# A kernel's beginning: prologue blocks folded into the first sublayer, transfers issued from two queues, and the opening's matmuls reordered

## The chip, the cores and the metric

The kernel runs on one core of a Trainium2 chip. The metric is the device time of one execution in microseconds (us); smaller is better. TensorE (PE) multiplies matrices and transposes by multiplying with an identity, VectorE (DVE), ScalarE (ACT) and GpSimd (POOL) work on elements, and SyncE (SP) issues transfers (DMA). Each engine runs its own instruction stream and waits for others on semaphores. The traces show TensorE's clock at two levels, 1.2 and 2.4 GHz; the granted clock of a stretch is given as a share of the higher one.

## What is computed

Input is `x`, 8 batches of 256 tokens with 256 features, in float32. A chain of residual sublayers is applied:

1. latent attention (16 heads): layer norm, projection to latents of 192 (query) and 64 (key and value) columns and 64 rotary columns, RMS norm of the latents, attention with a causal mask, output projection;
2. a linear layer whose weight is made ternary: `scale = mean(|W|)`, then every weight is rounded to one of -scale, 0, +scale;
3. a gated delta rule sublayer with short convolutions;
4. the ternary linear layer again;
5. latent attention again with other weights (in the code: call 1), and after it two smaller attention and feed-forward sublayers.

The kernel absorbs weights: the query weight and the key weight of a head are multiplied once into `wq0`, `wq1` (64 latent columns), and the value and output weights once into `w_out`, so that the attention works on latents. `layout` on the host only rearranges the inputs; it computes no product of them.

## The kernel before, in words

`build` makes its blocks one after the other. A `Block` gives each engine its stream; at its end all engines meet in a barrier, and the next block starts after it.

- `load_inputs` (line 134) is the first block: SP issues three transfers, the first batch `x[:, 0]`, the identity `ident` and the causal `mask`, all counted on one semaphore. DVE waits for all three and casts the identity to bfloat16 (line 150); the cast is used by the delta rule sublayer alone. POOL sets the constants `minus_half` and `ones_row`. The engines also prime the signals (each `Signal` is a semaphore with a counter that starts ahead, so that "the buffer of two iterations ago is free" holds at the beginning).
- `prime_signals` (line 279) is the second block: POOL alone primes the 13 preparation signals and 15 loop signals of the attention, 28 semaphore increments. Nothing else happens in it.
- `mla_sublayer` (line 332) with `call` = 0 is the third block: attention 0 with the ternary layer between its batches and the opening of the delta rule near its end. With `call` = 1 it is run again after the delta rule (there `after_attention` is false: each batch first goes through the ternary layer, then through attention 1).

Only the start of `mla_sublayer` matters here. SP issues its transfers in this order: `w_lat`, `norm_w` (the semaphore `small_in`), six tables (`small_in`), the ternary bias, the ternary weight (the float weight `w` in call 0, the finished weight `w_ste` from a DRAM buffer in call 1), the four query weights `q_nope`, `k_nope`, `q_pe0`, `q_pe1` (`queries_in`), `w_v`, `w_o` (`outputs_in`), then in call 0 the other seven batches and the weights of the next sublayer.

The dependent chain of call 0 for batch 0 is: layer norm (DVE L173 to L179, POOL power L197, DVE L189), transposes on PE (L213), copy on ACT (L664), latent projections (PE L656, ACT L673), squares (ACT L676, L678), root mean square (DVE L600 to L603, POOL L634 and L638), normalisation (DVE L612, L615) and the copy of the values (DVE L709). PE then transposes the normalised latents (`prep_late_pe`, L688 to L693). Beside this runs the preparation of weights:

- `query_weights_pe` (L544): 32 matmuls with 64 columns each, in two halves, into banks 1 to 4. A float32 matmul counts as two instructions in the profile. `query_weights_dve` (L554) copies the four banks to `wq0`, `wq1`. `query_weights_pool` (L561, L563) copies the rotary parts into them; it waits for `queries_in`.
- the ternary weight in call 0: row sum (DVE L512), total over partitions by one matmul with ones (PE L507) into bank 0, then eight DVE steps (L519 to L536). They use `w_out` as scratch (`z`, `up`, `down`, `wt`), so `output_weights_act` waits for the last step.
- `output_weights_pe` (L576) multiplies `w_v` and `w_o` of 16 heads into four banks (5, 6, 7, 1), and ACT copies them to `w_out` (L586).

PE's order in call 0 is: transposes and latents of batch 0, first half of the query weights, transposes of the latents, second half, total of the ternary weight, output weights, `weights_ready_pe` (a wait for all prepared weights), `project_pe` for head pairs 0 and 1 (L723, L724), then the loop over 64 head pairs: `scores_pe` (L762, L764), `project_pe` two pairs ahead, values times probabilities, output projection, transposes of the probabilities (L795). DVE turns each projection with the rotary tables (`rope_dve`, L730 and L736), POOL adds (L746), and ACT copies the other half (`abs_act`, L752). DVE takes masked maxima of the scores (L203) and ACT the exponentials (L783). In call 1 PE begins with the ternary layer of batch 0 (transposes, `ternary_y_pe` L491), and the ternary layer of batch 1 stands between the second half of the query weights and the output weights.

DVE's order in call 0 is: layer norm of batch 0, row sum, RMS norm, values, the eight steps, the four copies of the query weights, `rope_dve` 0 and 1, the loop. POOL's order is: two memsets (L1092, L1093), ones, power of the layer norm (L197), rotary part of the keys and the powers of the RMS norm, the copies L561 and L563, the rotary additions.

## Time and profile before

| what | us |
|---|---|
| median of 3 runs (3353.66 to 3354.33) | 3354.06 |
| the profiled execution, its own time | 3349.63 |
| span of that execution in the trace | 3347.8 |
| PE busy in the span | 3202.3 (96%) |
| DVE busy | 2408.9 (72%) |
| ACT busy | 1946.7 (58%) |
| POOL busy | 820.8 (25%) |

The mean granted clock of the profiled execution is 0.99. A line of the trace's timeline gives the start and the duration in us, engine, line of the kernel, operation, output and inputs, and in brackets how long the engine had been idle and what ended that. PE is the matmul, PEld its weight load, SPq the issue of a transfer on SP. Where equal operations follow each other, they are merged, and the duration is that of the whole group. A line of transfers gives the size and the median time from issue to landing.

### The profile page before, as it was taken

To read this page: it belongs to the slowest core of one execution; us is meant where nothing else is said; L and a number is where in the kernel's file an instruction comes from. 1 tells how busy PE (TensorE), PEld (TensorE's weight loads), DVE (VectorE), ACT (ScalarE), POOL (GpSimd) and SP (SyncE) were. 2 spreads that over 40 slices of the span, in tenths; PEclk is the share of its full clock that TensorE was granted. 3 is DMA by queue.
4 is the path that set the end of the run, shared out by engine and by line. 5 is a ranking of instruction groups with operands and counts; after the bars stand their busy time and mean duration, and the time that the engine had idled before them with its cause. 6 is when DMAs were issued, how large, how long until landed. Compare 5 with 4: busy or idle time off the path is not lost. (4 is left out here: it accounts for less than half of the span.)

```text
span 3347.8 us, 89254 instructions
## 1 busy us (share of the span) xinstructions
PE 3202.3 (96%) x34218; PEld 2635.2 (79%) x34218; DVE 2408.9 (72%) x7923; ACT 1946.7 (58%) x4769; POOL 820.8 (25%) x828
## 2 busy tenths in 40 slices
PE   6999989999999999999999969999889999999999
PEld 5888878888888888888888848888667777777787
DVE  4777778777788777788777637777666777777764
ACT  3555556666666666666666626565455555555553
POOL 2333322222222222222222323333210111111100
PEclk9999999999999999999999989999999999999999
DMA  6000000000000000000000040000000000000000
GB/s 241 1 1 1 1 8 27 21 21 17 17 18 25 18 25 18 15 21 21 21 22 18 12 162 1 1 1 1 1 1 1 2 1 1 1 5 5 5 8 10
DMA packets 51338, 66.84 MB, mean 20 GB/s; under 512 B 4962, under 2 KB 40291, under 8 KB 49379
## 3 DMA queue, kind: packets, MB, share of 16 engines
q1 hardware_dynamic: 50914, 61.13, 5.7%
q8 instruction: 274, 4.49, 0.5%
q14 instruction: 150, 1.22, 0.1%
HBM read 58.56 MB, written 2.56 MB: 18 GB/s over the span
## 5 line engine op out<-in xcount | busy, mean ns | idle before, releaser
L1404 DVE SCALAR_TENSOR_TENSOR d_acc<-d_raw,d_taps,d_acc 128x255 f32<-128x255 f32 x1116 | 627.4, 603 | 127.7 <-ACT d_raw L1392 114.5
L2482 ACT ACTIVATE s_probs<-s_probs,s_nmax 128x128 f32<-128x128 f32 (+1 forms) x768 | 287.0, 446 | 176.9 <-DVE s_nmax L203 176.2
L1659 ACT COPY d_power<-bank 128x768 f32<-128x768 f32 x320 | 259.0, 810 | 216.3 <-PE bank L1652 216.3
L203 DVE CUSTOM_DVE_ANT_0 s_probs<-bank,mask 128x128 f32<-128x128 f32 (+1 forms) x768 | 225.5, 349 | 108.0 <-PE bank L2463 107.9
L746 POOL TENSOR_TENSOR a_q<-a_rope 64x512 f32<-64x512 f32 x128 | 164.8, 1288 | 533.7 <-DVE a_recip L814 314.0
L1390 ACT ACTIVATE d_acc<-bank,d_tap_bias,d_taps 128x256 f32<-128x256 f32 x372 | 189.9, 561 | 162.9 <-PE bank L1368 156.4
L783 ACT ACTIVATE a_area<-a_area,a_nmax 128x128 f32<-128x128 f32 (+1 forms) x512 | 226.4, 443 | 85.7 <-DVE a_nmax L203 84.9
L203 DVE CUSTOM_DVE_ANT_0 a_area<-bank,mask 128x128 f32<-128x128 f32 (+1 forms) x512 | 159.0, 355 | 133.3 <-PE bank L764 130.8
L809 ACT COPY a_area<-bank 128x512 f32<-128x512 f32 (+1 forms) x260 | 137.2, 580 | 117.4 <-PE bank L800 117.4
L736 DVE TENSOR_TENSOR a_rope<-bank,a_sinT 32x512 f32<-32x512 f32 x256 | 177.4, 693 | 5.6
L1804 POOL TENSOR_TENSOR d_o_rs<-d_o_var,minus_half 128x4 f32<-128x4 f32 x64 | 69.6, 1087 | 402.3 <-DVE d_o_var L1798 402.3
L1432 POOL TENSOR_TENSOR d_qT<-d_acc,d_sigm 128x512 f32<-128x512 f32 x62 | 82.3, 1327 | 328.0 <-ACT d_sigm L1414 328.0
L723 PE MATMUL bank<-a_latT,a_wq 128*128 128x256 f32 x512 | 153.9, 382 | 6.9 <-DVE a_rope L736 4.5
L2490 PE MATMUL bank<-ident,s_probs 128*128 128x128 f32 x1152 | 147.6, 274 | 7.4 <-ACT s_probs L2482 4.7
L724 PE MATMUL bank<-a_qT,a_wq 128*128 128x256 f32 x512 | 153.7, 382 | 0.0
L764 PE MATMUL bank<-a_latT,a_q 128*128 128x256 f32 x512 | 153.6, 382 | 0.0
L2490 PEld LDWEIGHTS bank<-ident,s_probs 128*128 128x128 f32 x1152 | 130.3, 141 | 22.5 <-ACT s_probs L2482 15.2
L855 PE MATMUL bank<-a_w_out,a_area 128*128 128x256 f32 x512 | 145.6, 407 | 1.7 <-DVE a_area L844 1.7
L197 POOL TENSOR_TENSOR rstd<-var_eps,minus_half 128x2 f32<-128x2 f32 x64 | 46.1, 720 | 397.9 <-DVE var_eps L179 393.2
L1652 PE MATMUL bank<-d_power 64*64 64x64 f32 x4096 | 142.3, 217 | 0.0
L730 DVE TENSOR_TENSOR a_rope<-bank,a_cosT 64x512 f32<-64x512 f32 x128 | 88.9, 694 | 73.1 <-PE bank L724 71.2
L2590 PE MATMUL bank<-s_xT,m_w_up 128*128 128x256 f32 x512 | 140.3, 396 | 0.0
(287 smaller groups left out, 8621.7 us busy)
## 6 DMA issues: line engine op xcount, KB each, us to landing
d_alpha<-d_alpha_rows SPq DMA_DIRECT2D x64, 256.0 KB, 3.6
d_g_decay<-d_running_rows SPq DMA_DIRECT2D x32, 258.0 KB, 3.5
a_w_o<-in_a_w_o SPq DMA_DIRECT2D x2, 2048.0 KB, 16.8
a_area<-in_a_q_nope SPq DMA_DIRECT2D x2, 1536.0 KB, 8.2
x<-in_x SPq DMA_DIRECT2D x8, 256.0 KB, 16.8
d_wk<-in_d_wk SPq DMA_DIRECT2D x1, 2048.0 KB
d_wq<-in_d_wq SPq DMA_DIRECT2D x1, 2048.0 KB
d_wv<-in_d_wv SPq DMA_DIRECT2D x1, 2048.0 KB
```

The source lines that it names most:

```text
L203: return core.nc.vector.tensor_tensor_reduce(out=out, in0=scores, in1=core.mask[:, blocks], scale=-1.0, scalar=HIGHEST, op0=ALU.add, op1=A ...
L723: nc.tensor.matmul(out, wq0[:, h], latT[:, it % 2, 0], start=True, stop=False)
L724: last = nc.tensor.matmul(out, wq1[:, h], qT1[:, it % 2], start=False, stop=True)
L736: last = nc.vector.tensor_tensor(rope2[other], b_q[rows, :].rearrange("p (j t) -> p j t", j=2), sinT[rows].rearrange("p (j t) -> p j t", j ...
L746: nc.gpsimd.tensor_tensor(q[CL:P, n % 2], rope1[CL:P], rope2[CL:P], ALU.add)\
L764: nc.tensor.matmul(out[:, P:3 * P], q[:, n % 2, j, P:T], keys, start=False, stop=True, skip_group_check=True).then_inc(g.scores_in_psum.se ...
L783: last = nc.scalar.activation(own, own, ACT.Exp, scale=-1.0, bias=nmax[:, h % AHEAD, t:t + 1], accum_out=sums[:, n % 2, j, t:t + 1])
L1390: nc.scalar.activation(convolved(G, r)[:, j], b_proj[:, j * T:(j + 1) * T], ACT.Identity, scale=taps[:, r // 2, h, 3:4], bias=tap_bias[:, ...
L1404: last = nc.vector.scalar_tensor_tensor(out=convolved(G, r)[:, j, d:T], in0=raw[:, r % 2, j, 0:T - d], scalar=taps[:, r // 2, h, 3 - d:4 - ...
L1659: nc.scalar.copy(power[:], b_step[:, :, 0:3 * P]).then_inc(g.step_out, 1)
L2482: last = nc.scalar.activation(own, own, ACT.Exp, scale=-1.0, bias=nmax[:, s % 2, t, i:i + 1])
L2490: last = nc.tensor.transpose(heads[:, i, n * P:(n + 1) * P], probs[:, s % 2, i, n * P:(n + 1) * P], core.ident[:])
```

## The change

The two prologue blocks go. What they did moves into the first block of `mla_sublayer` (call 0): SP issues the first batch and the identity ahead of everything; the mask comes after the query weights; each input has a semaphore of its own, so DVE waits for the first batch alone before the layer norm, PE for the identity before the transposes, and DVE for the mask before the loop. PE primes the 28 signals. POOL sets its constants in the same stream. The cast of the identity moves to `set_up_dve`, near the end of attention 0.

Transfers come from two queues, in both calls. SP: `w_lat`, `norm_w`, query weights, now with the tables `cosT` and `sinT` among them, in call 0 the mask and the ternary bias, then the output weights. ACT: the four small tables and, in call 0, the ternary weight after them; in call 1 the finished ternary weight and the bias ahead of them.

The ternary weight's total is computed in bank 7 (`b_y`) instead of bank 0, right after the latents of batch 0. `output_weights_pe` comes after `project_pe` 0 and 1 and ACT's copies after `abs_act` 0 and 1, with bank 2 in place of bank 1; the wait for `w_out` moves to the first transposes of the loop.

The diff (lines left out are context):

```diff
@@ -66,7 +66,10 @@
         self.bank = [self.banks[:, i] for i in range(8)]
-        self.ready = ctx.enter_context(nc.semaphore("constants_ready"))
+        self.first_tokens_in = ctx.enter_context(nc.semaphore("first_tokens_in"))
+        self.ident_in = ctx.enter_context(nc.semaphore("ident_in"))
+        self.mask_in = ctx.enter_context(nc.semaphore("mask_in"))
+        self.constants_set = ctx.enter_context(nc.semaphore("constants_set"))
@@ -131,39 +134,35 @@
-def load_inputs(core):
-    nc, ins = core.nc, core.ins
-    with nc.Block() as block:
-        @block.sync
-        def _(sp):
-            sp.dma_start(core.x[:, 0], ins["x"][0]).then_inc(core.ready, 16)
-            sp.dma_start(core.ident[:], ins["ident"][:]).then_inc(core.ready, 16)
-            sp.dma_start(core.mask[:], ins["mask"][:]).then_inc(core.ready, 16)
-        @block.vector
-        def _(dve):
-            for s in (core.ln_stats, core.ln_mv, core.ln_var, core.ln_out):
-                s.prime(dve, 1)
-            core.x_updated.prime(dve, 2)
-            dve.wait_ge(core.ready, 16 * 3)
-            nc.vector.tensor_copy(core.ident_bf[:], core.ident[:])
-        @block.gpsimd
-        def _(pool):
-            core.ln_rstd.prime(pool, 1)
-            nc.gpsimd.memset(core.minus_half[:], -0.5)
-            nc.gpsimd.memset(core.ones_row[:], 1.0)
-        @block.scalar
-        def _(act):
-            core.xnT_ready.prime(act, 1)
-        @block.tensor
-        def _(pe):
-            core.xnT_in_psum.prime(pe, 1)
+def load_inputs_sp(core, sp):
+    sp.dma_start(core.x[:, 0], core.ins["x"][0]).then_inc(core.first_tokens_in, 16)
+    sp.dma_start(core.ident[:], core.ins["ident"][:]).then_inc(core.ident_in, 16)
+def prime_dve(core, dve):
+    for s in (core.ln_stats, core.ln_mv, core.ln_var, core.ln_out):
+        s.prime(dve, 1)
+    core.x_updated.prime(dve, 2)
+def prime_pool(core, pool):
+    core.nc.gpsimd.memset(core.minus_half[:], -0.5).then_inc(core.constants_set, 1)
+    pool.wait_ge(core.constants_set, 1)
+    core.nc.gpsimd.memset(core.ones_row[:], 1.0).then_inc(core.constants_set, 1)
+    pool.wait_ge(core.constants_set, 2)
+    core.ln_rstd.prime(pool, 1)
+def prime_pe(core, pe, prepared, looped):
+    core.xnT_in_psum.prime(pe, 1)
+    for s in prepared:
+        s.prime(pe, 1)
+    for s in looped:
+        s.prime(pe, 2)
@@ -277,19 +276,6 @@
-def prime_signals(core, prepared, looped):
-    with core.nc.Block() as block:
-        @block.gpsimd
-        def _(pool):
-            for s in prepared:
-                s.prime(pool, 1)
-            for s in looped:
-                s.prime(pool, 2)
@@ -301,6 +287,7 @@
         self.loaded, self.ones_set = sem("t_loaded"), sem("t_ones_set")
+        self.w_in = sem("t_w_in")
@@ -403,9 +390,9 @@
         tables = [(cos_tok[:], "cos_tok"), (sin_tok[:], "sin_tok"), (ms_scale[:], "ms_scale"),
-                  (q_scale[:], "q_scale"), (cosT[:], "cosT"), (sinT[:], "sinT")]
-        queries = [(q_nope, "q_nope"), (k_nope[:], "k_nope"), (q_pe0, "q_pe0"),
-                   (q_pe1, "q_pe1")]
+                  (q_scale[:], "q_scale")]
+        queries = [(q_nope, f"{tag}q_nope"), (k_nope[:], f"{tag}k_nope"), (q_pe0, f"{tag}q_pe0"),
+                   (q_pe1, f"{tag}q_pe1"), (cosT[:], "cosT"), (sinT[:], "sinT")]
@@ -440,7 +427,7 @@
             pool.wait_ge(*core.ln_out(ternary_at(b), NT))
-            pool.wait_ge(tern.loaded, 32 * (call + 1))
+            pool.wait_ge(tern.loaded, 16 if after_attention else 48)
@@ -485,7 +472,7 @@
             else:
-                pe.wait_ge(tern.loaded, 32 * (call + 1))
+                pe.wait_ge(tern.loaded, 48)
@@ -503,12 +490,11 @@
             pe.wait_ge(tern.row_sum_ready, 1)
-            pe.wait_ge(*g.latT_ready(-1, 2))
-            nc.tensor.matmul(b_prep[:, 0:1], ones[:], row_sum[:], start=True, stop=True)\
+            nc.tensor.matmul(b_y[:, 0:1], ones[:], row_sum[:], start=True, stop=True)\
...
         def ternary_row_sum_dve(dve):
-            dve.wait_ge(tern.loaded, 32)
+            dve.wait_ge(tern.w_in, 16)
@@ -516,7 +502,7 @@
             dve.wait_ge(tern.sum_in_psum, 1)
-            nc.vector.tensor_scalar(scale[:], b_prep[:, 0:1], 1.0 / (D * D), None, ALU.mult)\
+            nc.vector.tensor_scalar(scale[:], b_y[:, 0:1], 1.0 / (D * D), None, ALU.mult)\
@@ -563,13 +549,13 @@
-        OUT_BANKS = (5, 6, 7, 1)
+        OUT_BANKS = (5, 6, 7, 2)
...
             for n, bank in enumerate(OUT_BANKS):
-                if bank == 1:
-                    pe.wait_ge(g.wq_ready, 4 * call + 1)
+                if bank == 7 and after_attention:
+                    pe.wait_ge(tern.weight_step, 1)
@@ -586,9 +572,8 @@
-        def weights_ready_pe(pe):
+        def query_weights_ready_pe(pe):
             pe.wait_ge(g.wq_ready, staged)
-            pe.wait_ge(g.w_out_ready, staged)
@@ -788,6 +773,8 @@
             h = 2 * n + j
+            if h == 0:
+                pe.wait_ge(g.w_out_ready, staged)
@@ -870,18 +857,16 @@
             def _(sp):
+                if after_attention:
+                    load_inputs_sp(core, sp)
...
                     sp.dma_start(dst, ins[f"{tag}{name}"][:]).then_inc(g.small_in, 16)
-                for dst, name in tables:
-                    sp.dma_start(dst, ins[name][:]).then_inc(g.small_in, 16)
-                sp.dma_start(t_bias[:], ins["f0_b"].rearrange("(o n) d -> o n d", o=1)
-                             .broadcast_to([P, 1, D])).then_inc(tern.loaded, 16)
+                for dst, name in queries:
+                    sp.dma_start(dst, ins[name][:]).then_inc(g.queries_in, 16)
                 if after_attention:
-                    sp.dma_start(w[:], ins["f0_w"][:]).then_inc(tern.loaded, 16)
-                else:
-                    sp.dma_start(w_ste[:], tern.w_rows).then_inc(tern.loaded, 16)
-                for dst, name in queries:
-                    sp.dma_start(dst, ins[f"{tag}{name}"][:]).then_inc(g.queries_in, 16)
+                    sp.dma_start(core.mask[:], ins["mask"][:]).then_inc(core.mask_in, 16)
+                    sp.dma_start(t_bias[:], ins["f0_b"].rearrange("(o n) d -> o n d", o=1)
+                                 .broadcast_to([P, 1, D])).then_inc(tern.loaded, 16)
@@ -898,23 +883,26 @@
             def _(pe):
-                if not after_attention:
+                if after_attention:
+                    prime_pe(core, pe, g.prep, g.loop)
+                    pe.wait_ge(core.ident_in, 16)
+                else:
...
                 prep_lat_pe(pe, -1, range(NT))
+                if after_attention:
+                    ternary_sum_pe(pe)
...
                 query_weights_pe(pe, 1)
-                if after_attention:
-                    ternary_sum_pe(pe)
-                else:
+                if not after_attention:
...
                     ternary_y_pe(pe, 1)
-                output_weights_pe(pe)
-                weights_ready_pe(pe)
+                query_weights_ready_pe(pe)
...
                 project_pe(pe, 1)
+                output_weights_pe(pe)
@@ -959,7 +947,10 @@
             def _(dve):
-                if not after_attention:
+                if after_attention:
+                    prime_dve(core, dve)
+                    dve.wait_ge(core.first_tokens_in, 16)
+                else:
@@ -980,6 +971,8 @@
                 rope_dve(dve, 1)
+                if after_attention:
+                    dve.wait_ge(core.mask_in, 16)
@@ -1037,16 +1030,26 @@
             def _(act):
-                if not after_attention:
+                if after_attention:
+                    core.xnT_ready.prime(act, 1)
+                else:
+                    act.dma_start(w_ste[:], tern.w_rows).then_inc(tern.loaded, 16)
+                    act.dma_start(t_bias[:], ins["f0_b"].rearrange("(o n) d -> o n d", o=1)
+                                  .broadcast_to([P, 1, D])).then_inc(tern.loaded, 16)
+                for dst, name in tables:
+                    act.dma_start(dst, ins[name][:]).then_inc(g.small_in, 16)
+                if after_attention:
+                    act.dma_start(w[:], ins["f0_w"][:]).then_inc(tern.w_in, 16)
+                else:
...
                     ternary_copy_act(act, 1)
-                output_weights_act(act)
...
                 abs_act(act, 1)
+                output_weights_act(act)
@@ -1089,6 +1092,8 @@
             def _(pool):
+                if after_attention:
+                    prime_pool(core, pool)
@@ -1259,6 +1264,8 @@
         def set_up_dve(dve):
+            dve.wait_ge(core.ident_in, 16)
+            nc.vector.tensor_copy(core.ident_bf[:], core.ident[:])
@@ -2792,8 +2799,6 @@
         ternary = Ternary(ctx, core)
-        load_inputs(core)
-        prime_signals(core, mla.prep, mla.loop)
```

## Rows read from the trace of the kernel before

**Rows 1.** Busy time by 2 us stretches: columns PE, PEld, DVE, ACT, POOL, granted clock, DMA share, GB/s.
```profile
4.00:6.00 2.00, 0.00 (x0) 0.00 (x0) 0.23 (x1) 0.00 (x0) 0.00 (x0) 1.00 0.03 12
...
50.00:52.00 2.00, 2.00 (x8) 1.64 (x7) 0.00 (x0) 0.00 (x0) 0.79 (x1) 0.62 0.98 418
```

**Rows 2.** Timeline of the opening: start us, duration us, engine and line, idle before.
```profile
0.73 0.39 SPq L140 DMA_DIRECT2D x<-in_x  x1
...
7.61 1.80 POOL L1092 MEMSET a_wq<- 64x2048 f32 x1 [6.45 <-POOLq L282]
...
7.65 0.75 DVE L173 BATCH_NORM_STATS2 stats<-x 128x6 f32<-128x256 f32 x2 [2.74 <-PEq L282]
...
8.72 0.72 DVE L179 TENSOR_SCALAR var_eps<-mean_var 128x2 f32<-128x2 f32 x1
...
10.21 0.71 POOL L197 TENSOR_TENSOR rstd<-var_eps,minus_half 128x2 f32<-128x2 f32 x1
```

**Rows 3.** Transfers of the opening: first tokens' landing, an issue, output weights' landing.
```profile
DMA to landing us min/median/max: 2.6/16.8/17.1
...
12.25 0.43 SPq L884 DMA_DIRECT2D a_area<-in_a_q_nope  x1
...
a_w_o<-in_a_w_o SPq DMA_DIRECT2D x1, 2048.0 KB, 17.7
```

**Rows 4.** Timeline from the latents' norm to the first scores' maxima.
```profile
23.49 0.20 POOL L638 TENSOR_TENSOR a_inv_rms<-a_inv_rms,a_q_scale 128x4 f32<-128x4 f32 x1
...
24.90 0.23 DVE L709 COPY a_values<-a_k_tok 128x128 f32<-128x128 f32 x1
...
26.82 5.57 PE L544 MATMUL bank<-a_k_nope,a_area 128*128 128x64 f32 x32 [6.71 <-DMA a_rope<-in_a_q_pe]
...
26.82 1.04 POOL L561 COPY a_wq<-a_q 128x1024 f32<-128x1024 f32 x1 [3.13 <-DMA a_rope<-in_a_q_pe]
...
36.77 2.81 PE L576 MATMUL bank<-a_w_o,a_w_v 128*64 128x256 f32 x24
...
36.87 0.16 DVE L519 TENSOR_SCALAR a_t_scale<-bank 128x1 f32<-128x1 f32 x1 [11.75 <-PE bank L507]
...
40.95 2.46 DVE L554 COPY a_wq<-bank 128x512 f32<-128x512 f32 x4
...
43.51 1.04 PE L723 MATMUL bank<-a_latT,a_wq 128*128 128x256 f32 x2 [0.73 <-DVE a_wq L554]
...
47.15 0.69 DVE L730 TENSOR_TENSOR a_rope<-bank,a_cosT 64x512 f32<-64x512 f32 x1 [3.73 <-PE bank L724]
...
54.23 0.29 DVE L203 CUSTOM_DVE_ANT_0 a_area<-bank,mask 128x128 f32<-128x128 f32 x1
```

**Rows 5.** Two lines of VectorE over the whole span: duration ns min/median/max.
```profile
L1404 DVE SCALAR_TENSOR_TENSOR d_kT<-d_raw,d_taps,d_kT x12: 453/478/1498, 445.3 to 456.1; 128x255 f32<-128x255 f32 x4, 128x254 f32<-128x254 f32 x4, 128x253 f32<-128x253 f32 x4
...
L179 DVE TENSOR_SCALAR var_eps<-mean_var x64: 168/171/717, 8.7 to 3224.5; 128x2 f32<-128x2 f32 x64
```

**Rows 6.** The second attention call's start: timeline, and landing of the ternary weight.
```profile
1958.28 0.58 ACT L480 COPY xnT<-bank 128x512 f32<-128x512 f32 x1 [10.83 <-PE bank L213]
...
1962.26 3.50 PE L491 MATMUL bank<-a_t_w_ste,xnT 128*128 128x256 f32 x8 [4.02 <-DMA a_t_w_ste<-t_w_ste_rows]
...
a_t_w_ste<-t_w_ste_rows SPq DMA_DIRECT2D x1, 256.0 KB, 4.7
...
1989.41 3.67 PE L576 MATMUL bank<-a_w_o,a_w_v 128*64 128x256 f32 x32
...
1993.82 0.67 PE L723 MATMUL bank<-a_latT,a_wq 128*128 128x256 f32 x2 [0.73 <-issue]
...
2000.07 0.60 PE L764 MATMUL bank<-a_latT,a_q 128*128 128x256 f32 x2
...
2000.65 1.28 ACT L783 ACT_TABLE_LOAD   x1
...
2002.21 0.29 DVE L203 CUSTOM_DVE_ANT_0 a_area<-bank,mask 128x128 f32<-128x128 f32 x1
```

## The prediction

> **What bounds the kernel now.** I read the share of busy time first, then the 2 us stretches and the timeline of the two openings of the attention, then the landings. Over the whole span PE is the busiest engine; but the change touches only the first 60 us and the first 50 us of the second attention call, so the price has to be read there. In these stretches no engine is the bound: a chain of dependent steps is, and once the loop over head pairs runs, all that follows waits for data alone. So an opening that is shorter by some us moves the end by as many. The point that I follow is the start of the first masked maximum of the loop, 54.23 in call 0 [rows 4] and 2002.21 in call 1 [rows 6].
>
> Of call 0 the reader should see four things. The first batch was issued at 0.73 and lands 2.6 later, at 3.33 [rows 2, 3], but DVE reads it at 7.65, released by the priming on POOL and the barrier; in between the DMA engines are 3% busy [rows 1, 2]. PE starts the query weights at 26.82, when the last query transfer lands, though the values were copied at 24.90 [rows 4]. The ternary weight's steps begin at 36.87, 11.75 after DVE ran out of work, because the total stands behind both halves of the query weights on PE; the copies of the query weights (40.95, 2.46 long) queue behind these steps, and the first projection behind the copies, at 43.51 [rows 4]. And that projection takes 3.64 (until 47.15), where the same one in call 1 takes about 2.05: PE had idled, and the granted clock is 0.62 around 51 [rows 1, 4].
>
> **Call 0, part by part.**
>
> *Barriers and priming go.* DVE's layer norm starts at 3.35 instead of 7.65: 4.30 earlier. PE now makes the 28 increments, ACT five issues and a table load; both are waited for only after 6, so they cost nothing as long as they take less than 5 us (an issue takes 0.43 [rows 3]). The constants on POOL and its memsets (1.80 and a short one [rows 2]) start at about 0.8 and end before 4. Before, the last step of the norm's variance took 717 ns beside that memset, against a median of 171 [rows 5], and POOL reached the power only at 10.21. Now the variance starts at 3.35 + 1.07 = 4.42 and takes 0.17, and the power starts at 4.66: 5.55 earlier. From there to the end of the latents' norm nothing changes: POOL's last scale would end at 23.69 - 5.55 = 18.14, and the norm at 24.90 - 5.55 = 19.35. The identity and `w_lat` are issued within the first 2 us; nothing waits for them.
>
> *Queries.* The first query transfer was issued at 12.25 and PE started at 26.82, 14.57 later [rows 3, 4]. It is now fifth on SP, 0.73 + 4 x 0.45 = 2.55. The bias and the ternary weight no longer stand ahead, which helps; the latents' weight is still under way and two tables of 128 KB are added, which hurts. I take the same 14.57 and get 17.1, with 15 and 19 as ends. PE's row from 26.82 to the output weights at 36.77 is 9.95 without a gap, of which 0.3 is the total that has moved ahead; so the query weights end at 17.1 + 9.65 = 26.75. That includes the transposes of the latents, whose inputs are there by then.
>
> *The total moved.* It costs PE 0.3 at about 15, where PE waits for the queries anyway. Bank 7 is free then. DVE no longer idles for it: the ternary steps follow the values' copy. From 36.87 to 40.95 they take 4.08, and the copies 2.46 [rows 4].
>
> *A new collision.* POOL's two copies (1.04 and about the same [rows 4]) ran while DVE idled. Now they start at 18.2 together with DVE's norm, whose operations read two tensors from SBUF. What that costs is seen elsewhere: an operation of this form has a median of 478 ns and a maximum of 1498 [rows 5], so it can wait a whole POOL operation out. The bounds are 0 and 2.07. I take 2.07, since the same scale releases both engines and POOL's copy is one step from starting. The norm then ends at 21.4, the values at 21.65, the ternary steps at 25.75, the copies at 28.2, and the first projection starts at 28.3 instead of 43.51. The last bank of PE's own chain (26.75 + 0.6) is ready just before. The Trainium skill ("SBUF — State Buffer", SBUF: two separate sides) says that whoever starts first holds the shared port for the whole instruction; were DVE first, POOL would wait, the projection would start at 27.4, and the sum would be 0.9 better.
>
> *Output weights moved behind the projections.* From the first projection to the first maximum call 1 needs 2002.21 - 1993.82 = 8.39 [rows 6]: projection, rotary, projection, rotary, at 2.05 and 2.13 each. Now the 32 output matmuls, 3.67 [rows 6], stand on PE between the second projection and the scores, beside the second rotary, and the scores of one head (0.60 and the 128-column pair, 0.8) come after. New chain at the high clock: 2.05 + 2.13 + 2.05 + 3.67 + 0.8 + 0.1 = 10.8. The output weights' inputs took 17.7 from issue; even at that they land well before 36. With the low clock for the first projection alone it is 12.4; with the low clock throughout 3.64 x 2 + 2.13 + 7.34 + 1.6 = 18.35. PE idles 1.5 us before the first projection and had idled before it in the old kernel, so I take 12.4. The first maximum comes at 28.3 + 12.4 = 40.7: **13.5 us** earlier. ACT's four copies trail PE and end before the first exponential; DVE's wait for the mask, issued at about 5.5, is over long before.
>
> **Call 1.** PE waited for the ternary weight until 1962.26, while ACT's copy ended at 1958.86 [rows 6]. The weight, 4.7 from issue, was the tenth issue of SP; it is now ACT's first, the bias the second, 4.2 and 3.3 earlier. If both land by 1958.9, PE starts 3.3 earlier. ACT's six issues (2.7) end before its first copy at 1958.28. Then the first projection need not wait for the output weights and their copies: 1993.82 - 1989.41 = 4.4. The chain to the first maximum grows from 8.39 to 10.8: minus 2.4. In this call ACT also loads a table (1.28) ahead of the exponentials; it was hidden under the rotary, and now comes after the output copies: minus 0.5. Sum: 3.3 + 4.4 - 2.4 - 0.5 = **4.8 us**, with 1.5 (weight not earlier) and 5.3 as ends.
>
> **The cast** of the identity, 0.23 on DVE near the end of attention 0, I cost at nothing: it lies beside PE's work there. Without this cover it is 0.23, and 1.5 if it meets a POOL operation.
>
> **Sum.** 13.5 + 4.8 = 18.3. The profiled execution took 3349.63, 4.4 below the median of the runs shown; 3349.63 - 18.3 = 3331.3, and against the median 3354.06 - 18.3 = 3335.8.
>
> **Rivals.**
> - *The clock stays high and the port costs nothing.* For it: call 1 runs its projections at the high level after a similar gap. Then 1.6 and 0.9 more: 3333.3. Chance 0.17.
> - *The clock is low through the output weights.* For it: 0.62 at 50 to 52 right after a projection and a pause [rows 1]. Then 18.35 instead of 12.4: gain 12.3, 3341.7. Chance 0.12.
> - *The transfers are the bound, not their issue.* From 50 to 52 the DMA engines are 98% busy [rows 1], and if the ternary weight shares them with latents' and query weights, it lands no earlier in call 1 (3.3 lost), and the queries land at 19 in call 0 (1.3 lost): 3340.4. The Trainium skill ("DMA: Bandwidth & Descriptors", Issuing engines are not separate DMA queues) says that transfers of several engines interleave on the same DMA engines, and that a second issuer saves issue time only. Against it: the stretch from 4 to 6 is empty. Chance 0.10.
> - *The opening does not start at once.* If engines begin the long block late, or priming is slow on PE, up to the 4.3 of the barriers stay: 3340.1. Chance 0.04.
> - *Slower.* The clock falls in places that are high today. The shift moves all later work against the moments at which the clock changes. One us at 1.2 GHz does half a us of work at 2.4, so the change loses by more than 6.7 us only from (18.3 + 6.7) x 2 = 50 us of additional low clock on; at 60 us the time is 3354.06 - 18.3 + 30 = 3365.8. The whole mean clock is 0.99, and nothing in the edited parts lengthens PE's pauses. Chance 0.02.
>
> **Numbers.** The forecast has 0.55, time 3335.8. The low end takes the best of both calls (16.0 + 5.3) and 3 for the clock elsewhere: about 3330. The high end takes the low clock case with some of the lost transfers: 3344. A difference of 0.2% is 6.7 us, about what a measurement of this kernel can tell from none. Every case but the last gains 12 or more; combined they can fall under 6.7. So faster 0.95, same 0.03, slower 0.02.
>
> **What would show it.** DVE's first statistics at 3.4 and the power at 4.7; the query weights on PE at about 17; DVE's norm stretched by POOL's copies; no idle time of DVE before the ternary steps; the first projection at 28, and its duration 3.6 or 2.0; the output weights as one group of 3.7 between second projection and scores; the first maximum at 41. In call 1 the wait ahead of the first ternary matmuls (4.02 [rows 6]) down to 0.7, and everything from the block's begin to the first maximum shorter by 4.8. I am wrong if the loop's first maximum comes after 47, or if later stages lose what the openings gain.

## The result, and the profile after

The changed kernel takes 3333.38 us (median of 4 executions, 3332.42 to 3341.8) beside 3353.86 of the kernel before in the same job. The ratio is 0.9945, with a 95% interval from 0.9929 to 0.9961: a gain of 0.55%, and the interval lies wholly below 1. The profiled execution took 3332.42, against 3349.63 before: 17.2 less in its own time, 17.4 less in the span. The forecast was 18.3 less.

The page of the changed kernel: span, busy times, and the queue that is new.

```profile
span 3330.4 us, 89230 instructions
...
PE 3200.7 (96%) x34218; PEld 2635.6 (79%) x34218; DVE 2409.5 (72%) x7923; ACT 1948.7 (59%) x4769; POOL 821.4 (25%) x828
...
q10 hardware_dynamic: 1584, 0.93, 0.1%
```

The shares say nothing of the change; as ahead of the prediction, the openings have to be read. This is the timeline of the changed kernel's call 0, the places of [rows 2, 4].

```profile
0.73 0.39 SPq L139 DMA_DIRECT2D x<-in_x  x1
0.80 0.38 ACTq L1040 DMA_DIRECT2D a_cos_tok<-in_cos_tok  x1
...
3.88 0.75 DVE L172 BATCH_NORM_STATS2 stats<-x 128x6 f32<-128x256 f32 x2 [3.88 <-DMA x<-in_x]
...
4.96 0.17 DVE L178 TENSOR_SCALAR var_eps<-mean_var 128x2 f32<-128x2 f32 x1
5.21 0.71 POOL L196 TENSOR_TENSOR rstd<-var_eps,minus_half 128x2 f32<-128x2 f32 x1 [1.32 <-DVE var_eps L178]
...
8.67 2.93 PE L641 MATMUL bank<-a_w_lat,xnT 128*128 128x384 f32 x4 [0.78 <-DMA a_q_scale<-in_q_scale]
...
16.52 5.57 PE L530 MATMUL bank<-a_k_nope,a_area 128*128 128x64 f32 x32 [1.14 <-DMA a_sinT<-in_sinT]
...
18.71 1.04 POOL L547 COPY a_wq<-a_q 128x1024 f32<-128x1024 f32 x1
18.81 1.15 DVE L597 SCALAR_TENSOR_TENSOR a_q_tok<-a_lat,a_inv_rms,a_norm_w 128x192 f32<-128x192 f32 x1 [1.42 <-POOL a_inv_rms L623]
...
19.88 1.05 DVE L600 SCALAR_TENSOR_TENSOR a_k_tok<-a_lat,a_inv_rms,a_norm_w 128x64 f32<-128x64 f32 x1
...
21.63 0.15 DVE L505 TENSOR_SCALAR a_t_scale<-bank 128x1 f32<-128x1 f32 x1
...
25.70 2.47 DVE L540 COPY a_wq<-bank 128x512 f32<-128x512 f32 x4
28.23 0.70 PE L708 MATMUL bank<-a_latT,a_wq 128*128 128x256 f32 x2 [1.65 <-DVE a_wq L540]
...
30.26 0.69 DVE L715 TENSOR_TENSOR a_rope<-bank,a_cosT 64x512 f32<-64x512 f32 x1 [2.09 <-PE bank L709]
...
34.38 3.67 PE L562 MATMUL bank<-a_w_o,a_w_v 128*64 128x256 f32 x32
...
39.05 0.29 DVE L202 CUSTOM_DVE_ANT_0 a_area<-bank,mask 128x128 f32<-128x128 f32 x1 [2.44 <-issue]
```

Three readings. The layer norm waits for its data alone, and the variance takes 0.17 again instead of 0.72. The ternary steps follow the values' copy without the pause of 11.75 [rows 4]. The first masked maximum comes at 39.05 instead of 54.23, 15.2 earlier. At 8.67 the latents on PE, released by a copy before, are now released by the landing of `q_scale`, a table of 2 KB that they do not read. PE idles 0.78 there and idled 0.77 before, so in this execution it costs next to nothing. The query weights at 16.52 are released by the landing of `sinT`, a table that they do not read either; their own last transfer had landed at about 15.2. That delay costs nothing here, since DVE's copies, not PE, release the first projection.

In call 1 the wait for `q_scale` is the larger one: PE idles 1.54 ahead of the latents, and idled 0.77 there before. The timeline of the changed kernel's second attention call, whose block begins at 1938.28 (it began at 1953.24 before):

```profile
1944.69 3.75 PE L478 MATMUL bank<-a_t_w_ste,xnT 128*128 128x256 f32 x8 [1.40 <-DMA a_t_bias<-in_f_b]
...
1954.47 2.93 PE L641 MATMUL bank<-a_w_lat,xnT 128*128 128x384 f32 x4 [1.54 <-DMA a_q_scale<-in_q_scale]
...
1972.58 0.59 PE L708 MATMUL bank<-a_latT,a_wq 128*128 128x256 f32 x2
...
1982.95 1.28 ACT L768 ACT_TABLE_LOAD   x1
1983.19 0.29 DVE L202 CUSTOM_DVE_ANT_0 a_area<-bank,mask 128x128 f32<-128x128 f32 x1 [2.33 <-PE bank L749]
```

And the landings there (line, KB, us from issue to landing):

```profile
a_t_bias<-in_f_b ACTq DMA_DIRECT2D x1, 128.0 KB, 5.9
...
a_ms_scale<-in_ms_scale ACTq DMA_DIRECT2D x1, 2.0 KB, 12.4
a_q_scale<-in_q_scale ACTq DMA_DIRECT2D x1, 2.0 KB, 13.8
```

From the block's begin to the first maximum, call 1 takes 44.91 instead of 48.97: 4.06 less. At that point the whole is 2002.21 - 1983.19 = 19.0 ahead. At the first row of the output it still is (2985.2 against 3004.2); at the end of the span it is 17.4, after one stretch of 3.4 us at the low clock near 3103 that the trace of before does not have.

### The profile page after: what moved, and what is told of

Its sections match the earlier page's. It is cut to its first block and busy times, and to the rows that moved or that the text cites. A ratio compares the mean times of both kernels' runs of the same rounds, so it can differ in the third digit from the quotient of the medians.

```text
span 3330.4 us, 89230 instructions
## 1 busy us (share of the span) xinstructions
PE 3200.7 (96%) x34218; PEld 2635.6 (79%) x34218; DVE 2409.5 (72%) x7923; ACT 1948.7 (59%) x4769; POOL 821.4 (25%) x828
## 5 line engine op out<-in xcount | busy, mean ns | idle before, releaser
L1640 PE MATMUL bank<-d_power 64*64 64x128 f32 x3072 | 139.4, 271 | 0.0
```

## The experiments

The landmark in all of them is the first masked maximum: of call 0 from the span's start (before 54.23, changed 39.05), of call 1 from its block's begin (before 48.97, changed 44.91). Times are medians. The kernel before stood at 3354.24 in the first job (again, prologue_back, sum_late, out_first), 3352.16 in the second (split_waits, act_copies, interleave, one_queue) and 3354.42 in the third (warm_clock, barriers_alone, combined, combined_warm).

**again** is the changed kernel itself, as the mark for the others of its job.

> The changed kernel once more, unedited, to see how far its runs spread. Theory A (chains shortened: the gain is fixed by what each step waits for): 3331 to 3335 in nearly all runs, and the first maximum of call 0 at 39.0 to 39.2. Rival B (part of the gain hangs on when small transfers land among big ones): the spread is wider than the 0.8 us of the kernel before, and the time of the first maxima moves by more than 1 us from one profile to the next.

Measured: 3337.68 (5 executions, 3332.86 to 3339.07), ratio 0.9948 [0.9936, 0.9961]. In call 0 the first maximum came at 39.63, outside the 39.0 to 39.2 that were expected: 0.6 later, though the power came 0.3 earlier (4.92). Between them stands the small table:

```profile
9.25 1.01 PE L641 MATMUL bank<-a_w_lat,xnT 128*128 128x384 f32 x1 [1.66 <-DMA a_q_scale<-in_q_scale]
```

In call 1 the first maximum came at 52.74 instead of 44.91. Stretches of 10 us from 1939 on (columns as in [rows 1]), first of the changed kernel as first profiled:

```profile
1939.00:1949.00 10.00, 4.87 (x12) 3.24 (x12) 2.29 (x8) 0.59 (x1) 3.54 (x4) 0.50 0.91 319
...
1959.00:1969.00 10.00, 8.82 (x69) 7.64 (x68) 3.93 (x16) 2.50 (x11) 3.45 (x7) 0.82 1.02 391
1969.00:1979.00 10.00, 7.06 (x41) 5.46 (x41) 5.12 (x9) 1.43 (x3) 4.35 (x4) 1.00 0.83 308
```

then of the same kernel as again:

```profile
1959.00:1969.00 10.00, 10.00 (x48) 8.48 (x47) 3.35 (x15) 2.50 (x11) 3.23 (x6) 0.50 1.02 392
1969.00:1979.00 10.00, 9.32 (x41) 7.94 (x42) 2.85 (x6) 0.58 (x1) 3.28 (x3) 0.50 0.90 338
```

The clock granted from 1959 to 1969 is 0.82 in one execution and 0.50 (1.2 GHz) in the other, with 69 and 48 matmuls done in the same 10 us. At the first maximum of call 1 the two are 7.8 apart, at the end of the span 5.3 (3330.4 and 3335.7), so this opening makes the difference between these two, and later stages give some of it back. Of the five executions of again, the one with a mean clock of 0.991 has a span of 3330.9, the two with 0.988 have 3336.5 and 3337.1. The expected 3331 to 3335 did not come in nearly all runs, and rival B, with a wider spread and moving landmarks, fits better, except that the clock moves them more than the landings do. The spread is not the change's own, though: in the same job the kernel before ran from 3349.49 to 3358.82. A single profile of this program is therefore good for its waits and no better than some 9 us for its time.

One caution for what follows. Over the first 20 us the granted clock of the rows reads 1.00 in every trace, and yet four matmuls of 128x384 took 2.93 there, where warm_clock below has 1.56 for the same four. In some runs it reads 1.00 through slow projections too. So where the text says "low clock" of call 0's opening, it reads this from the lengths of equal matmuls; a granted clock is given where a row shows it.

**prologue_back** puts the two barriers and the priming on POOL back, with the first loads in the first block; the rest of the change stays.

```
+def prologue(core, prepared, looped):
+    with nc.Block() as block:
...
+            load_inputs_sp(core, sp)
+            sp.dma_start(core.mask[:], ins["mask"][:]).then_inc(core.mask_in, 16)
...
+    with nc.Block() as block:
...
+            core.xnT_in_psum.prime(pool, 1)
+            for s in prepared:
+                s.prime(pool, 1)
+            for s in looped:
+                s.prime(pool, 2)
...
+        prologue(core, mla.prep, mla.loop)
```

> The two prologue blocks are back ahead of the first sublayer (first batch, identity and mask in one block, POOL primes 28 signals in the next); everything else as in the changed kernel. Theory A: DVE's statistics start at 7.6 instead of 3.9, the memset of POOL meets the variance again, the power starts at 10.2 instead of 5.2, and the whole chain shifts by 5.0: first maximum at 44, time 5.0 longer (about 3338.4). Rival B (the opening is bound by the transfers of the queries, and those run anyway once issued): the queries are issued 6.0 later, the query weights start at 22.5, and the first maximum shifts by 6. Rival C (barriers were free, the gain came from the order on PE): less than 2 us longer.

Measured: 3347.87 (10 executions, 3340.39 to 3359.04), 0.9984 [0.9974, 0.9994], 10.2 above again where 5 were expected; the first maximum at 53.17, 14.1 later than with the change, the power 4.8 later. That is more than the barriers. The trace shows a second loss:

```profile
18.78 2.93 PE L676 MATMUL bank<-a_w_lat,xnT 128*128 128x384 f32 x4 [6.14 <-DMA a_q_scale<-in_q_scale]
...
a_q_scale<-in_q_scale ACTq DMA_DIRECT2D x1, 2.0 KB, 10.0
```

With the block's transfers issued all at once behind the barrier, the small table landed after 10.0, and PE waited 6.14 for it. The third loss is the clock: the granted one falls to 0.77 between 28 and 30 and to 0.50 from 30 on, the second half of the query weights takes 5.41 (3.21 in the change), and from the first projection to the first maximum it takes 15.40 instead of 10.82, 4.6 more. So this run mixes three causes, and does not price the barriers.

**barriers_alone** has the same prologue, but all transfers of the attention on SP's queue, the tables ahead of the large ones.

> The two prologue blocks back, on top of the kernel with all transfers on one queue. Theory A (the barriers and the priming are worth 5.0, and the rest of what the run with prologue and two queues lost was the small tables' late landing, which the one queue does not have): power at 9.8, latents at 13.2 to 13.4 with no wait for a table, query weights at 23, first maximum 5 to 7 later than the 38.8 of the one-queue kernel; time 5 to 7 above its 3332.8. Rival (the prologue itself costs 10 or more): latents late again, first maximum beyond 50.

Measured: 3340.76 (4, 3338.39 to 3346.51), 0.9964 [0.995, 0.9977]. Against one_queue below, which differs by the prologue alone, the first maximum comes at 44.62 instead of 38.76. That is the price of the two blocks as a whole: 5.9 at the first maximum, 5.6 of them at the power, as expected (5 to 7). Most of it stands ahead of DVE's first statistics, which start at 7.78 instead of 3.44; DVE was through with its own wait at 4.91 and then idled 2.81 to the next block. How much of this is the barriers, how much the priming, and how much the wait for all three inputs of the first block, this run does not separate. The times, 3340.76 against 3332.8, come from two jobs and are 8 apart, with intervals of the two ratios that touch; the trace carries the reading.

**one_queue** leaves ACT without transfers; the tables stand ahead of the queries, in call 1 behind the ternary weight and the bias.

```
             def _(sp):
...
+                if not after_attention:
+                    sp.dma_start(w_ste[:], tern.w_rows).then_inc(tern.loaded, 16)
+                    ...
                 for dst, name in early:
                     sp.dma_start(dst, ins[f"{tag}{name}"][:]).then_inc(g.small_in, 16)
+                for dst, name in tables:
+                    sp.dma_start(dst, ins[name][:]).then_inc(g.small_in, 16)
...
             def _(act):
...
-                for dst, name in tables:
-                    act.dma_start(dst, ins[name][:]).then_inc(g.small_in, 16)
```

> All transfers of the opening on SyncE's queue: in call 0 first batch, identity, latents' weight, norm weight, four tables, ternary weight, queries; in call 1 finished ternary weight, bias, then as before. ScalarE issues none. Theory A (the second queue saves SyncE 0.45 per issue but lets small transfers wait among big ones): in call 0 the queries are issued 2.3 later and the query weights start at 17.5 to 19 instead of 16.5 to 16.9; the small tables land within 3 us again. In call 1 latents no longer wait for a table (+14.6 to +15). Together within 1 us of the changed kernel at the same clock. Rival (the second queue is worth its 5 issues of 0.45): 2.3 us longer or more.

Measured: 3332.8 (4, 3331.62 to 3333.84), 0.9941 [0.9924, 0.9958]; first maximum at 38.76 in call 0, 50.01 in call 1 with the low clock. On one queue the small table of call 1 lands soon, and no wait for it is left in either call:

```profile
a_q_scale<-in_q_scale SPq DMA_DIRECT2D x1, 2.0 KB, 3.6
```

In call 0 the table took 3.1. The kernel issues the queries 2.4 later than the change does, at 4.97, and PE starts on them at 17.20 instead of 16.52, in both kernels when `sinT` has landed. The kernel before issued them at 12.25 and started at 26.82. So the second queue is not what brought the gain: that the issues come some 7 us earlier, with no barrier ahead of them, is enough without it. The Trainium skill ("DMA: Bandwidth & Descriptors", Issuing engines are not separate DMA queues) says that a second issuing engine saves issue time only; the runs agree, and add that it can cost: 3.6 against 13.8 for the same 2 KB.

**split_waits** keeps both queues and cuts the waits down to what is read: a semaphore of its own for `w_lat`, and one for the ternary weight apart from the bias.

```
- pe.wait_ge(g.small_in, early_in)
+ pe.wait_ge(g.lat_w_in, 16 * (call + 1))
...
- pe.wait_ge(tern.loaded, 48)
+ pe.wait_ge(tern.ste_in, 16)
```

> The latents' weight has a semaphore of its own, so PE no longer waits for the four small tables before the latent projections; and in the second attention call PE waits for the finished ternary weight alone, not for the bias too. Nothing is issued in another order. Theory A (the tables of ScalarE's queue land 6 to 14 us after issue because they share the DMA engines with megabytes of query weights, and PE waits for them): latents start 0.1 to 0.8 earlier in call 0 and at +14.6 to +15 instead of +15.9 to +16.2 in call 1, ternary matmuls at +5.7 instead of +6.3; 1.5 to 2 us shorter at the same granted clock. Rival (PE is late there for another reason, the wait only happens to end then): no change at these places.

Measured: 3335.08 (4, 3333.58 to 3339.0), 0.9951 [0.9936, 0.9966]. Both waits are gone: the first ternary matmuls start at +5.69 from the block's begin instead of +6.41, the latents at +14.96 instead of +16.19. The first maximum does not follow: +46.29, with the low clock in the way. In call 0 nothing was freed: from the power to the latents it takes 3.43 as in the change (3.46), and the first maximum comes at 40.47 behind output weights that took 4.84 instead of 3.67. The 1.2 us that were freed in call 1 are real and smaller than what the clock moves.

**sum_late** puts the total of the ternary weight back behind both halves of the query weights.

```
                 prep_lat_pe(pe, -1, range(NT))
-                if after_attention:
-                    ternary_sum_pe(pe)
                 query_weights_pe(pe, 0)
...
                 query_weights_pe(pe, 1)
+                if after_attention:
+                    ternary_sum_pe(pe)
```

> The total of the ternary weight goes back behind both halves of the query weights on PE, still in bank 7; everything else as in the changed kernel. Theory A (DVE's queue of ternary steps and copies sets the first projection): the total ends at about 26.9, the ternary steps start at 27.0 instead of 21.6, the first projection at 33.6 instead of 28.2, first maximum 5.4 later, and 1.6 more if PE's longer pause brings the low clock. Time 3338.8 to 3340.5. Rival (PE's chain of query weights sets the projection, DVE's steps are beside it): under 1 us.

Measured: 3342.23 (5, 3339.84 to 3347.24), 0.9966 [0.9954, 0.9978], 4.6 above again. Its PE and DVE rows:

```profile
24.19 5.41 PE L530 MATMUL bank<-a_k_nope,a_area 128*128 128x64 f32 x32
29.53 0.59 PE L493 MATMUL bank<-a_t_row_sum,a_t_ones 128*128 128x1 f32 x2
...
36.76 0.80 PE L708 MATMUL bank<-a_latT,a_wq 128*128 128x256 f32 x1 [6.64 <-DVE a_wq L540]
...
30.16 0.16 DVE L505 TENSOR_SCALAR a_t_scale<-bank 128x1 f32<-128x1 f32 x1 [8.61 <-PE bank L493]
```

DVE idles 8.61 for the total, PE then 6.64 for DVE. The first projection comes 8.5 later than in the change, and the first maximum 11.7 (50.75), since the projections now ran at the low clock. Not all of the 8.5 is the move's. The query weights started 0.83 later (17.35), and their second half took 5.41 instead of 3.21, at the low clock, 2.2 more. What is left, about 5.5, is the move itself, as expected (5.4), and about as much as the two blocks. Whether PE's longer pause brings the low clock behind it, as the 1.6 of the expectation had it, one execution can't show; it was low here before that pause. In the times the intervals of this ratio and of again's still touch (0.9954 and 0.9961), so the idle rows carry this, not the time.

**out_first** puts the output weights ahead of the query projection again, in banks that are free there, with ACT's copies moved along.

```
-        OUT_BANKS = (5, 6, 7, 2)
+        OUT_BANKS = (5, 6, 7, 1)
...
+                output_weights_pe(pe)
                 query_weights_ready_pe(pe)
                 project_pe(pe, 0)
                 project_pe(pe, 1)
-                output_weights_pe(pe)
```

> Output weights ahead of the first projections again in both calls, with their ACT copies and the wait for all of them, banks 5, 6, 7, 1; everything else as in the changed kernel. Theory A: in call 0 they fill PE's pause from 26.6 to 28.2 and delay the projection to about 31.1, while the chain from projection to first maximum falls from 10.8 to 8.4: 0.5 longer. In call 1 the projection comes 4.4 later, the chain is 2.3 shorter, the table load hides again: 1.8 longer. Together 2.3 longer, about 3335.7. Rival (the order is what brought the gain): 5 us or more longer. Rival (order is free): within 0.5.

Measured: 3335.3 (4, 3332.15 to 3337.98), 0.994 [0.9925, 0.9955]; first maximum at 38.70, 0.35 earlier than with the change. The projection starts 2.1 later (30.31), but nothing stands between it and the scores. The 0.35 is not the order's: the query weights had started 0.30 earlier (16.22), and from there to the first maximum it takes 22.48 here and 22.53 in the change. So in call 0 this part of the change is worth nothing on its own. In call 1 the first maximum came at +53.30, 0.56 behind again's, both with the low clock; 1.8 were expected. The time is 2.4 below again where 2.3 above was expected, inside the spread: the times of the two orders cannot be told apart.

**interleave** splits the output weights, and ACT's copies of them with it: half after each projection, beside the rotary.

```
  project_pe(pe, 0)
+ output_weights_pe(pe, (0, 1))
  project_pe(pe, 1)
- output_weights_pe(pe)
+ output_weights_pe(pe, (2, 3))
```

> Two of the four groups of output weights go between the first and the second projection, where PE waits 2.2 us for the rotary products; the other two stay behind the second. Theory A (output weights behind the second projection hold the scores up): the chain from first projection to first maximum shortens from 10.8 to about 9.0 in call 0, and by 1.5 to 1.8 in call 1; 3 to 3.5 us shorter at the same clock. Rival (the rotary on VectorE ends last anyway): no gain, since 8.4 is the floor and table load and copies on ScalarE take the rest: under 1 us.

Measured: 3332.64 (4, 3327.8 to 3336.56), 0.9941 [0.9926, 0.9956]. Nothing in the time that can be told from the change. The chain does show it: in call 1, at the high clock, it takes 8.89 from the first projection to the first maximum instead of 10.61, 1.7 less, as expected (1.5 to 1.8), and the maximum comes at +43.53. In call 0 it came at 41.80: PE idled 2.37 for `q_scale` ahead of the latents, and the first projection ran at the low clock.

**act_copies** moves the two copies of the queries' rotary part from POOL to ACT.

```
- nc.gpsimd.tensor_copy(wq0[:, :, CL:P], q_pe0).then_inc(g.pe_copied, 1)
+ nc.scalar.copy(wq0[:, :, CL:P], q_pe0).then_inc(g.pe_copied, 1)
```

> The two copies of the rotary query weights move from GpSimd to ScalarE, which is idle then. Theory A (VectorE's operations with two SBUF operands stand still while GpSimd copies): in call 0 the norm takes 1.15 from its first operation to the values' copy instead of 2.7, and the ternary steps start 1.5 earlier; the first projection follows by 1.0 to 1.5, when PE's own chain takes over; first maximum about 38.0. Rival (the norm is stretched by something else, such as the DMA writes into SBUF): the stretch stays at 2.7 and nothing moves.

Measured: 3337.07 (4, 3330.82 to 3341.24), 0.9953 [0.9938, 0.9968]. The timeline of its norm and of what followed:

```profile
19.15 0.42 DVE L595 SCALAR_TENSOR_TENSOR a_q_tok<-a_lat,a_inv_rms,a_norm_w 128x192 f32<-128x192 f32 x1 [1.41 <-POOL a_inv_rms L621]
19.48 0.28 DVE L598 SCALAR_TENSOR_TENSOR a_k_tok<-a_lat,a_inv_rms,a_norm_w 128x64 f32<-128x64 f32 x1
...
23.56 5.41 PE L530 MATMUL bank<-a_k_nope,a_area 128*128 128x64 f32 x32
...
29.01 0.68 DVE L540 COPY a_wq<-bank 64x512 f32<-64x512 f32 x1 [1.21 <-PE bank L530]
29.75 0.79 PE L706 MATMUL bank<-a_latT,a_wq 128*128 128x256 f32 x1 [0.78 <-DVE a_wq L540]
```

The collision is confirmed: the norm's operations take 0.42 and 0.28 instead of 1.15 and 1.05, and the norm 1.17 (19.15 to 20.32) instead of 2.68. But the first projection is 1.5 later than in the change, not 1.0 to 1.5 earlier: PE did the second half of the query weights in 5.41 instead of 3.21, at the low clock, and now DVE's copies waited for PE. The first maximum came at 43.83 where about 38.0 was expected, behind projections at the low clock. The two chains were within a microsecond of each other, as the prediction's 26.75 + 0.6 had it.

**warm_clock** adds matmuls whose results nobody reads (12 of 128 columns ahead of the first transposes of call 0, 5 of 384 in call 1, and a few in each later pause of PE in the openings).

```
+ warm_pe(pe, 12)
  ...
+ nc.tensor.matmul(b_s[1][:, 0:cols], core.ident[:], src[:, 0:cols], start=True, stop=True)
```

> The changed kernel, with matmuls added that compute nothing that is read (identity times identity in call 0: 12, 2, 5 and 2; identity times mask in call 1: 5, 1, 4, 1 and 2), into bank 4 before it is first used, at the places where PE waits in the two openings. Theory A (the spread of 5 to 8 us between runs and profiles of one kernel is the granted clock of the second attention call's opening, 10 or 27 us of low level after 1964): with PE kept busy the low level there goes; ternary matmuls of call 1 take 1.9 instead of 3.75, each latent projection 1.6 instead of 2.9, first maximum at +38 to +41 instead of +44.9 or +52.7, and the runs lie within 2 us of each other, 5 to 10 below the changed kernel's. Rival (spread comes from landings of transfers): low level gone or not, the spread stays and the time does not fall.

Measured: 3332.89 (5, 3332.05 to 3335.36), 0.994 [0.9927, 0.9952]; first maximum at 42.70 in call 0, +41.60 in call 1. The times spread by 3.3 and lie at the low end of the changed kernel's, not 5 to 10 below. In call 1 there is a gain (latents in 1.56 instead of 2.93, and 3.3 at the first maximum, 11 against again), though PE idled 2.17 for `q_scale`. In call 0 the first maximum is 3.65 later. PE's own timeline:

```profile
5.23 5.36 PE L630 MATMUL bank<-ident 128*128 128x128 f32 x24 [5.23 <-issue]
10.43 0.60 PE L212 MATMUL bank<-ident,xn 128*128 128x128 f32 x4
...
28.59 1.22 PE L715 MATMUL bank<-a_latT,a_wq 128*128 128x256 f32 x2 [3.04 <-DVE a_wq L540]
```

PE gets to its first matmul at 5.23 only, does the added ones at half rate at first and reaches the real transposes at 10.43 instead of 6.79, 3.6 later. But from there it works at full rate: the latents take 1.53 and 1.56 instead of 2.93 each, the query weights start at 16.90 instead of 16.52, and the first projection at 28.59 instead of 28.23. All but 0.36 of the delay is made up. The loss comes behind it: the granted clock fell to 0.86 between 26 and 28, when PE idled 3.04 ahead of the projection, and is 0.50 from 28 to 30. The projection took 3.8 (28.59 to 32.41) instead of 2.03, and all from there to the first maximum 14.11 instead of 10.82, 3.3 more.

**combined** takes one_queue, split_waits, act_copies and interleave together.

> One queue, split waits, ScalarE's copies of the rotary query weights, and interleaved output weights together. Theory A (the four act on different waits): norm in 1.15, ternary steps at 19.6 to 20.5, first projection at 26.5 to 27.5, first maximum at 35 to 36.5 if the clock is high there; ternary matmuls of call 1 at +5.7, latents at +15.0, first maximum at +42 to +43 with high clock and +50 with low. 3 to 5 us below the changed kernel at the same clock: 3328 to 3332. Rival (they meet in one chain that ends at the same time): no more than the one-queue kernel's 3332.8.

Measured: 3327.69 (5, 3325.22 to 3332.81), 0.9923 [0.9911, 0.9936], just under the expected 3328 to 3332. The norm takes 1.17 again. But the first projection comes at 29.69 instead of 26.5 to 27.5, and the first maximum at 38.78 instead of 35 to 36.5. The trace says why:

```profile
18.39 5.58 PE L531 MATMUL bank<-a_k_nope,a_area 128*128 128x64 f32 x32 [3.59 <-DMA a_sinT<-in_sinT]
...
27.87 0.69 DVE L541 COPY a_wq<-bank 128x512 f32<-128x512 f32 x1 [2.99 <-PE bank L531]
...
a_k_nope<-in_a_k_nope SPq DMA_DIRECT2D x1, 512.0 KB, 8.0
...
a_sinT<-in_sinT SPq DMA_DIRECT2D x1, 128.0 KB, 10.4
```

What these matmuls read was issued by 5.42 and had landed at 13.4; they waited by a shared count for the last table, issued at 7.95, until 18.39, and DVE in turn idled for PE. A semaphore of their own for these two transfers was not tried. The chain behind the first projection is 9.09 (expected 9.0). In call 1 the first maximum comes at +42.67, inside the +42 to +43 that were expected.

**combined_warm** adds the matmuls of warm_clock to it.

> The combined kernel with the added matmuls of the warm_clock run. Theory A: both gains add, first maximum of call 0 at 32 to 35, of call 1 at +36 to +39; 3318 to 3325. Rival (low level is not lifted by the added matmuls, or they hold up real work): not below the combined kernel.

Measured: 3324.06 (4, 3321.29 to 3326.68), 0.9909 [0.9893, 0.9924]. This is the best version: its interval lies below that of the changed kernel (0.9929 to 0.9961), while it touches that of combined, so what the added matmuls give on top is likely and not shown. The first maximum comes at 37.95 and at +39.94, both behind the expected 32 to 35 and +36 to +39; the time is inside the expected 3318 to 3325. Its call 1:

```profile
1942.36 1.99 PE L479 MATMUL bank<-a_t_w_ste,xnT 128*128 128x256 f32 x8
...
1949.39 1.53 PE L649 MATMUL bank<-a_w_lat,xnT 128*128 128x384 f32 x4
...
1975.85 0.29 DVE L202 CUSTOM_DVE_ANT_0 a_area<-bank,mask 128x128 f32<-128x128 f32 x1 [0.60 <-PE bank L757]
```

The first ternary matmuls take 1.99 instead of 3.75, the latents 1.53 instead of 2.93. In call 0 the matmuls delay the transposes here too (10.48), but PE starts the query weights only at 19.35, when the last table of the shared count lands (the queries had landed by 16.2), so the delay lies inside that wait. Matmuls in call 1 alone, and fewer of them in call 0, were not tried.

## Why the prediction was right

The time, 3333.4, lies 2.4 below the forecast of 3335.8 and inside the range; the median of again, 3337.7, lies 1.9 above it. By its steps, whose numbers come from the changed kernel's first profile where no run is named:

*Barriers and priming.* Right: the power at 5.21, forecast 4.66. The 0.55 is the first tokens' landing, 3.1 after issue instead of 2.6 [rows 3], with a second queue's tables beside it; on one queue it is back at 4.76. The variance took 0.17 as said. That the two blocks carry about 5.5 is shown by barriers_alone (5.6 at the power against the 5.55 of the forecast). The step held PE's 28 increments for free under 5 us: the first instruction of PE is at 5.23 in warm_clock and 5.22 in combined_warm, so the margin was thinner than the text let one think (PE's first work was due at 6.8).

*Queries.* 16.52 against 17.1. Right within its ends: 14.57 was taken from the first issue on, 13.93 came. What ended the wait was a table, `sinT`, and not the queries.

*The total.* Right: DVE no longer idles ahead of the ternary steps. sum_late shows the idle time directly and puts the move at about 5.5.

*The collision.* Right in kind and place, 1.5 (2.68 - 1.17) instead of 2.07. Two of DVE's four operations met one copy each; they took 2.20 together where act_copies has 0.70. The step charged both copies whole, but the operations' own time counts against that. POOL was first, at 18.71 against 18.81. The Trainium skill's rule that whoever starts first holds the shared port for its whole instruction ("SBUF — State Buffer", SBUF: two separate sides) agrees: DVE's first operation ended at 19.96, just behind POOL's first copy (19.75), the second at 20.93, just behind POOL's second (20.86), and act_copies takes the effect away.

*First projection.* 28.23 against 28.3.

*From there to the first maximum.* This is the term that was mis-sized in call 0: 12.4 was taken, for one projection at the low clock, and 10.8 came (28.23 to 39.05), the chain at the high clock exactly. So call 0 gained 15.2 instead of 13.5. The reason given for the low level, that PE idles 1.5 before the projection, is not borne out: PE idled 1.65 there and the projection was fast. The other level is no less real: prologue_back, sum_late, interleave, act_copies and warm_clock took 3.6 to 3.8 for this projection. In the first four the second half of the query weights, ahead of the pause, had already taken 5.41. What decides between the levels in a given execution is not settled by these runs.

*Output weights behind the projections.* The forecast gave the move 4.4 in call 1 and charged 2.4 for the longer chain behind it. It came in call 1: the chain from the first projection to the first maximum is 10.61 instead of 8.39, 2.2 more, and the projection need not wait 4.5 for output weights. The table load behind the copies, charged with 0.5, costs 0.4, but at the first exponential (1.06 instead of 0.68 behind the maximum) and not at the landmark. In call 0 out_first shows that the balance is nil.

*Call 1.* 4.06 against 4.8; the 0.5 of the table load is not in the landmark, so 5.3 is what 4.06 has to be held against. The step that failed is "if both land by 1958.9": the weight landed in 4.0, but the bias in 5.9, and the wait counts both, which left 1.40 where 0.7 was expected, and PE started 2.6 earlier instead of 3.3. The text priced the early landing of what moved first on ACT's queue and not the late landing of what came last on it: four tables, on which PE's latents wait by a shared count. They landed 9.5 to 13.8 after issue, and the latents lost 0.77 there (1.54 instead of 0.77). It was not foreseen in either call, and neither was the query weights' wait for `sinT` in call 0. split_waits and one_queue each remove the latents' wait.

*The sum.* 15.2 + 4.1 = 19.3 by the landmarks, 19.0 on the clock of the trace at the first output, 17.4 at the end. The last 1.6 fit the 3.4 us at the low clock near 3103, which cost half of themselves. That the sum came within 1 us of the forecast is in part luck: 1.6 more in call 0 from a clock that the forecast had low, and 1.6 lost late in the span, which it had nowhere, cancel.

*The rivals.* High clock without port cost (3333.3) is nearest in time, but by a wrong pair: the clock was high and the port cost was there. The low clock through the output weights came in no run as a whole: they took 3.67 in most, warm_clock included, 4.68 in prologue_back, 4.84 in split_waits and 4.26 in sum_late, never 7.34. The transfers as the bound: queries at 16.52 speak against it, the late tables for a part of it; with queries at 19, the prediction's own chain (19 + 9.65 + 0.6 = 29.25) loses 1.0 and not 1.3. Slower by clock: no run of the change came near it, though the effect it builds on is the largest source of spread.

## What to carry to other kernels

When an opening is a chain of dependent steps, look for what stands in it by order alone: a barrier ahead of data that has landed, a small result queued behind large work. One semaphore count for several transfers waits for the last of them: give what is read first its own, or issue the tables ahead of the megabytes on the same queue. combined shows this lever still unused at the query weights. And before a gain of a few microseconds is believed, compare the granted clock of the stretches and the lengths of equal matmuls in them, since here nine executions of one kernel differ by 9 us, and the kernel before by as much.

## What was not expected of the hardware

- A transfer of 2 KB as the sixth on ACT's queue, issued while SP's queue carried megabytes, landed 13.8 us after its issue; ahead of them on one queue it took 3.6, and 2.2 in the kernel before. The second queue delayed the small ones and brought the queries of call 0 only 0.7 earlier, for an issue 2.4 earlier.
- The clock granted in call 1's opening differed between two executions of the same kernel (0.82 and 0.50 in one stretch, 1.00 and 0.50 in the next), which is 7.8 us at the first maximum. With matmuls without a purpose it was at the high level there in the one profile of warm_clock; ahead of call 0 they started at half rate themselves and delayed the transposes by 3.6, of which faster real matmuls left 0.4 at the first projection.
- The granted clock of the rows reads 1.00 over the first 26 us both in the change and in warm_clock, though equal matmuls take nearly twice the time in the one (latents 2.93 and 1.56, half of the query weights 5.57 and 3.07).
- The same 2 KB table ended an idle time of PE of 0.78 to 2.37 in call 0 of five profiles with the same transfers (0.78 in the change, 0.85 in sum_late, 1.29 in act_copies, 1.66 in again, 2.37 in interleave).
- PE's first instruction came at 5.2 from the span's start in warm_clock and combined_warm, the two runs that gave it work so early, where SP issued its first transfer at 0.73.
